# One-hot tiles built block by block with a column of codes as the scalar, and node degrees counted later

## The chip, the cores and the metric

The kernel runs on one NeuronCore of a Trainium2 chip. The metric is device time in microseconds of one execution, from start to end of the program; lower is better. The engines that matter are TensorE (PE), VectorE (DVE), ScalarE (ACT), GpSimd (POOL) and the DMA queue of SyncE (SP). They run side by side, each with its own instruction stream, and meet at semaphores.

## The reference

A graph network on 3125 nodes with 512 features and 53125 directed edges (`src`, `dst`, sorted by `dst`). Two parts, each followed by a residual and a layer norm:

```python
# part 0: three mean-aggregation layers
deg = segment_sum(ones, dst); inv_deg = 1 / clip(deg, 1)
h = x
for l in range(3):
    neigh = segment_sum(h[src], dst) * inv_deg[:, None]
    h = h @ Ws_self[l] + neigh @ Ws_neigh[l] + bs[l]
    if l != 2: h = relu(h)
x = layernorm(x + h)
# part 1: per edge: a filter MLP on 20 attributes, times gathered 4*32 features and
# 4 angular values, summed into the node idx_i = src, two small products, layer norm
```

## The kernel before

The nodes are cut into 25 tiles of 125. Part 0 sums neighbours with a dense adjacency count matrix: for each destination tile a plane of 125 source rows x (25 tiles x 125) in bf16, kept in DRAM as `adj`. The product `h @ Wn` is split into a high and a low f16 half (`table`), so that one aggregation of a tile is 25 x 2 matmuls of 512 columns (line 1122).

**Building the planes.** Edges of five consecutive destination nodes form a block of at most 128 edges; 25 blocks make one destination tile. For each edge there are two codes: the source row within its tile (0 to 124) and source tile x 5 + node within the block (0 to 124). DVE makes for a tile two one-hot arrays of 128 edges x 25 blocks x 125, `oh_b` (`one_hot_rows`, line 1546) and `oh_c` (`one_hot_codes`, line 1552), each in one instruction that compares two broadcast operands. PE multiplies them block by block (line 993, 25 matmuls of 125 columns for a tile, in seven groups in PSUM), ACT evicts each group (line 1253) and SP stores the plane.

**Order of the work.** Three written-out loops set the order on every engine.

- First stage, `for w in range(25)`: node tile w is transposed and multiplied with the first layer's two weight matrices (`product(w, 0)` and `product(w, 1)`, line 964, four steps of 512 columns each). DVE takes the row maximum and scale (lines 1568 to 1574), the low half (line 1581, after ACT's high half of line 1242) and the own part plus bias (`own_part`, line 1607). The plane builder runs `LAG` = 6 node tiles behind: `builder_of(w)` is w - 6. On DVE iteration w makes the one-hots of the tile that PE multiplies in w + 1. On PE the seven groups of blocks stand after the first seven of the eight steps of the two products.
- Aggregation, `for k in range(75)`: k = 0 to 24 is layer 0, and so on. PE does the 50 matmuls of tile k and, in between, the next layer's transposes and products. The last six planes are built here (one-hots in k = 0 to 4). DVE also scales the adjacency plane (`scale`, line 1561), adds mean and own part (`mean_plus_state`, line 1614), and in k = 1 to 17 sorts edges by source for part 1 (`bin_numbers`, `count_bins`, `bin_starts`, `place_bins`, `places_first`, `places_last`).
- Part 1: POOL scatters the sorted edges' rows to DRAM (line 820), and later gathers messages (lines 856 and 825) that DVE, ACT and PE work on.

**The head.** `chunks`, `first_edges`, `codes_first` (w = 2) and `codes_second` (w = 3) make the codes on DVE from rows that POOL gathered. `codes_second` also compares 125 x 3200 values (line 1474) and sums them (line 1476) for the node degrees. SP stores the degrees and reads them back as rows at w = 4, PE transposes them at w = 5 (line 1072), and `degrees_and_rounds` turns them into `inv_deg`. That same function derives from a flag whether a general path is needed (`rounds_i`); each engine then loads this value into a register and branches over the general path (`general`), which these inputs never take. On PE the branch stands ahead of the products of w = 5.

Of the kernel before, what the change touches and what calls it, by code (L numbers as in the profile page):

```python
# [5 lines left out]
BF16 = mybir.dt.bfloat16  # L6
# [5 lines left out]
P = 128  # L12
# [74 lines left out]
def gnn_kernel(nc, x, src, dst, src_n, pay, ws, wn, bs, w_in, w1, b1, w2, b2, wf1, wf2, out):  # L87
# [40 lines left out]
    inv_deg = sb("inv_deg", [P, TILES])  # L128
    deg_row = sb("deg_row", [TILES, TN])
# [23 lines left out]
    place_i = sort.take(P, [CH], I32)  # L153
    early = Region(sort_sb[:, :], 7 * CH * 4)
# [52 lines left out]
    col_b = high.take(P, [GB, EP], BF16)  # L207
    col_c = high.take(P, [GB, EP], BF16)
# [4 lines left out]
    part_b = alias.take(EP, [GB, P])  # L213
    part_c = alias.take(EP, [GB, P])
    in_node = alias.take(EP, [GB, NODES, P], BF16)
    node_deg = alias.take(EP, [GB, NODES])
# [28 lines left out]
    gfirst = pre.take(EP, [GB], I32)  # L245
    falls = oh_b[0].rearrange("p a d -> p (a d)")[0:EP, 0:EC]
# [192 lines left out]
    BLOCKS_AT = (1, 4, 8, 10, 15, 18, 21)  # L439

# [88 lines left out]
    with nc.Block() as block:  # L529

        @block.sync
        def _(sp):
# [96 lines left out]
            for k in range(KC):  # L629
                sp.dma_start(weights[0][:, 0, k, :], wn[0, k * P:(k + 1) * P, :]).then_inc(s_w0[k], 16)  # L630
            load_weights(0, 1)
            load_x(1)
# [4 lines left out]
            for w in range(TILES):  # L637
# [15 lines left out]
                if w == 4:  # L653
                    sp.wait_ge(s_degn, 1)
                    sp.dma_start(bass.AP(degrees.tensor, 0, [[NODES, EP], [NODES * EP, GB], [1, NODES]]), node_deg[:, :, :]).then_inc(s_degst, 16)
                    sp.wait_ge(s_degst, 16)
                    sp.dma_start(deg_row[:, :], degrees.rearrange("(t d) -> t d", d=TN)).then_inc(s_degld, 16)
# [262 lines left out]
        def _(pe):  # L920
# [61 lines left out]
            def multiply_blocks(tb, j):  # L982

                if j == 0:
                    pe.wait_ge(s_ohb, tb + 1)
                    pe.wait_ge(s_ohc, tb + 1)
# [9 lines left out]
            def transpose_codes():  # L996
                pe.wait_ge(s_codes, 1)
                for g in range(GB - 1):
                    pe.transpose(p_b[0][:, g * EP:(g + 1) * EP], part_b[:, g, :], ident[0:EP, 0:EP])
                    last = pe.transpose(p_b[1][:, g * EP:(g + 1) * EP], part_c[:, g, :], ident[0:EP, 0:EP])  # L1000
                last.then_inc(s_ctp[0], 1)
                pe.wait_ge(s_cols, 2)
                pe.transpose(p_b[0][:, 0:EP], part_b[:, GB - 1, :], ident[0:EP, 0:EP])
                pe.transpose(p_b[0][:, P:P + EP], part_c[:, GB - 1, :], ident[0:EP, 0:EP])
                pe.matmul(p_b[1][0:1, 0:1], flags[0:EP, 2:3], ones32[0:EP, 0:1], start=True, stop=True).then_inc(s_ctp[1], 1)
# [59 lines left out]
            for w in range(TILES):  # L1065
                if w + 1 < TILES:
                    transpose_x(w + 1)
                tb = builder_of(w)
                if w == LAG - 1:
                    pe.wait_ge(s_meta, 1)  # L1070
                    pe.wait_ge(s_degld, 16)
                    pe.transpose(p_b[1][0:TN, 0:TILES], deg_row[:, :], ident[0:TILES, 0:TILES]).then_inc(s_degt, 1)
                    general(pe, general_counts)

                def blocks_between(step):
                    if tb is not None and step < PARTS:
                        multiply_blocks(tb, step)

                product(w, 0, blocks_between)
                product(w, 1, blocks_between)  # L1080
                if w == LAG - 2:
                    transpose_codes()
# [146 lines left out]
        def _(act):  # L1229
# [25 lines left out]
            def columns():  # L1255
                act.wait_ge(s_ctp[0], 1)
                for b, col in enumerate((col_b, col_c)):
                    act.activation(col[:, 0:GB - 1, :], p_b[b][:, 0:(GB - 1) * EP].rearrange("p (g e) -> p g e", e=EP), ACT.Copy).then_inc(s_cols, 1)
                act.wait_ge(s_ctp[1], 1)
                for b, col in enumerate((col_b, col_c)):  # L1260
                    act.activation(col[:, GB - 1, :], p_b[0][:, b * P:b * P + EP], ACT.Copy).then_inc(s_cols, 1)

            transposed(0, ACT.Copy)
            for w in range(TILES):
                if w + 1 < TILES:
                    transposed(w + 1, ACT.Copy)
                if w == LAG - 2:
                    columns()
# [4 lines left out]
                row_hi(w)  # L1273

# [722 lines left out]
```

## Time and profile before

| | |
|---|---|
| median of 3 runs | 1993.61 us (1992.96 to 1994.01) |
| profiled execution | 1993.22 us |
| its span, first to last instruction | 1991.4 us |
| outside the span | 1.8 us |
| PE busy | 1870.8 us (94%) |
| DVE busy | 1284.2 us (64%) |
| POOL busy | 1088.7 us (55%) |
| ACT busy | 591.3 us (30%) |
| mean granted TensorE clock | 0.978 |

A row of a timeline gives the start, the duration, the engine, the source line, the operation, what is written and read, the shapes, and in brackets how long the engine was idle before it and who ended that. Durations of neighbouring instructions of one engine overlap a little, so the time that an instruction costs its engine is the distance from its start to the next start, called its pitch below. The timeline merges like instructions (x4, x16). A PE product of one step shows as two records.

### The profile page before, as it was taken

How to read it: one execution, taken by the hardware profiler on the slowest of the kernel's cores; microseconds unless marked ns; L12 is line 12 of the kernel's file. 1: busy time of each engine (PE TensorE's matmuls, PEld its weight loads, DVE VectorE, ACT ScalarE, POOL GpSimd, SP SyncE). 2: the span in 40 equal slices, each digit the busy share in tenths (PEclk: the TensorE clock that was granted, in tenths of full speed). 3: DMA queues.
4: the chain of work that ended last, by engine and by line, in shares of the span. 5: the costliest groups of instructions: out<-in, count | busy, mean ns of one | idle time of the engine just before them, and what ended most of it. 6: DMA issues, size and time to landing. Idle time of an engine off the chain costs nothing. (4 is left out here: it accounts for less than half of the span.)

```text
span 1991.4 us, 23719 instructions
## 1 busy us (share of the span) xinstructions
PE 1870.8 (94%) x8447; PEld 1195.1 (60%) x8447; DVE 1284.2 (64%) x1989; ACT 591.3 (30%) x1380; POOL 1088.7 (55%) x1057
## 2 busy tenths in 40 slices
PE   7799989999999999999999999999994988989996
PEld 3344446555555555555555556666663777878885
DVE  6899999767884333333333334555542888989997
ACT  1355533200000000000000000111112767778884
POOL 4000000000007788878887888568887777777773
PEclk9899999999999999999999999999996999999998
DMA  4155454422223324323232324555654334333341
GB/s 148 59 174 183 157 190 149 150 88 68 91 87 110 87 78 136 110 86 95 93 99 83 94 67 140 163 174 193 199 165 129 98 101 119 107 98 112 111 114 49
DMA packets 112345, 236.72 MB, mean 119 GB/s; under 512 B 28406, under 2 KB 52627, under 8 KB 112224
## 3 DMA queue, kind: packets, MB, share of 16 engines
q1 hardware_dynamic: 77152, 179.50, 27.6%
q0 software_dynamic: 35072, 55.66, 10.4%
q8 instruction: 70, 1.15, 0.2%
q14 instruction: 51, 0.42, 0.1%
HBM read 159.94 MB, written 75.11 MB: 118 GB/s over the span
## 5 line engine op out<-in xcount | busy, mean ns | idle before, releaser
L1122 PE MATMUL low<-table,abuf 125*125 125x512 f16 x3750 | 845.7, 380 | 4.8 <-DVE abuf L1561 4.8
L1122 PEld LDWEIGHTS low<-table,abuf 125*125 125x125 bf16 x3750 | 506.1, 137 | 301.1 <-issue 29.4
L964 PE MATMUL mid<-wbuf,h_t 128*125 128x512 f32 x1200 | 558.7, 602 | 4.3 <-DVE st_out L1607 2.8
L820 POOL DMA_INDIRECT by_src<-scat_row,sort x416 | 487.5, 1172 | 126.1 <-issue 118.9
L825 POOL DMA_INDIRECT table<-msg_table,wbuf x294 | 315.5, 1073 | 91.0 <-issue 87.6
L964 PEld LDWEIGHTS mid<-wbuf,h_t 128*125 128x125 f32 x1200 | 214.4, 189 | 208.7 <-issue 198.9
L812 POOL TENSOR_TENSOR scat_row<-scat_row 128x64 f32<-128x64 f32 x26 | 16.1, 618 | 557.2 <-DVE sort L1727 556.7
L1156 PE MATMUL low<-table,wbuf 128*125 128x256 f32 x900 | 220.4, 396 | 56.4 <-DVE table L1857 55.9
L1614 DVE SCALAR_TENSOR_TENSOR y<-low,inv_deg,st_in 125x512 f32<-125x512 f32 x75 | 56.3, 750 | 326.0 <-PE low L1122 205.7
L1561 DVE TENSOR_TENSOR abuf<-abuf,row_scale 125x3125 bf16<-125x3125 bf16 (+3 forms) x84 | 256.5, 3059 | 3.5 <-DMA abuf<-adj 3.5
L1238 ACT ACTIVATE h_t<-mid 128x500 f32<-128x500 f32 x100 | 58.5, 585 | 583.2 <-PE mid L934 436.9
L1156 PEld LDWEIGHTS low<-table,wbuf 128*125 128x125 f32 x900 | 173.3, 196 | 90.6 <-DVE table L1857 60.5
L856 POOL DMA_INDIRECT sort<-msg_table,sort x156 | 185.3, 1188 | 60.5 <-issue 60.5
L1242 ACT ACTIVATE table<-mid,row_inv 125x512 f16<-125x512 f32 x75 | 51.5, 686 | 427.7 <-DVE row_inv L1573 427.7
L1568 DVE TENSOR_REDUCE row_max<-mid 125x1 f32<-125x512 f32 x75 | 51.6, 688 | 175.2 <-PE mid L964 174.8
L1351 ACT ACTIVATE table<-table,wbuf 128x128 f32<-128x128 f32 x450 | 139.3, 388 | 58.6 <-DVE table L1845 57.6
L1253 ACT ACTIVATE table<-top 125x500 bf16<-125x500 f32 (+1 forms) x175 | 117.2, 693 | 98.5 <-PE top L993 98.2
L993 PEld LDWEIGHTS top<-table 128*125 128x125 bf16 x625 | 59.4, 138 | 92.7 <-issue 56.0
L1134 PE MATMUL mid<-w_sb,wbuf 97*128 97x384 f32 (+2 forms) x450 | 112.7, 387 | 2.3 <-issue 2.3
L1581 DVE SCALAR_TENSOR_TENSOR table<-mid,row_inv,table 125x512 f16<-125x512 f32 x75 | 56.3, 751 | 56.8 <-ACT table L1242 54.6
L1546 DVE TENSOR_TENSOR table<-table,node_iota 128x3125 bf16<-128x3125 bf16 x25 | 85.2, 3407 | 2.2 <-issue 2.2
L1552 DVE TENSOR_TENSOR table<-table,node_iota 128x3125 bf16<-128x3125 bf16 x25 | 85.2, 3408 | 0.0
(214 smaller groups left out, 1658.1 us busy)
## 6 DMA issues: line engine op xcount, KB each, us to landing
abuf<-adj SPq DMA_DIRECT2D x75, 781.2 KB, 4.8
adj<-table SPq DMA_DIRECT2D x25, 781.2 KB, 4.6
states<-st_out SPq DMA_DIRECT2D x75, 256.0 KB, 2.0
st_in<-states SPq DMA_DIRECT2D x75, 256.0 KB, 4.9
table<-early_rows SPq DMA_DIRECT2D x25, 384.0 KB, 6.7
early_rows<-sort POOLq DMA_DIRECT2D x24, 384.0 KB, 3.2
by_src<-scat_row,sort POOLq DMA_INDIRECT x416, 2.2
by_src<-blank SPq DMA_DIRECT2D x25, 252.0 KB, 4.4
```

The costliest lines, as they stand in the source:

```text
L820: pool.indirect_dma_start(out=by_src, out_offset=bass.IndirectOffsetOnAxis(ap=place_i[:, k * PIECE + j:k * PIECE + j + 1], axis=0), in_=sc ...
L825: pool.indirect_dma_start(out=rows[:, j, :], out_offset=None, in_=msg_table[:, :], in_offset=bass.IndirectOffsetOnAxis(ap=win[:, j, PAY_DS ...
L856: pool.indirect_dma_start(out=e_rows[s % 3][:, j, :], out_offset=None, in_=msg_table[:, :], in_offset=bass.IndirectOffsetOnAxis(ap=idx, ax ...
L964: last = pe.matmul(to[0:TN, :], h_t[i % 2][:, k, :], weights[l % 2][:, a, k, :], start=k == 0, stop=k == KC - 1)
L1122: last = pe.matmul(p_agg[k % 2][0:TN, :], a_tile[k % 3][:, a, :], table[ps % 2][0:TN, a, h, :], start=a == 0 and h == 0, stop=a == TILES - ...
L1134: last = pe.matmul(w[:, (b * BLK + lo) * G:(b * BLK + hi) * G], filters[b], w2_sb[:, lo:hi, :].rearrange("k a b -> k (a b)"), start=True, ...
L1156: last = pe.matmul(p_acc[0:TN, :], hot32[:, g * GS + j, :], msg[n % 2][:, j, :], start=g == 0 and j == 0, stop=g == NG - 1 and j == GS - 1)
L1253: act.activation(to, of, ACT.Copy).then_inc(s_blke, 1)
L1351: last = act.activation(msg[n % 2][:, j, 0:G], av[n % 2][:, j, :], ACT.Copy, scale=win_p[t % 3][:, g * GS + j, PAY_Y:PAY_Y + 1])
L1546: dve.tensor_tensor(oh_b[tb % 2], col_b.rearrange("p g e -> p (g e)")[:, tb * BLOCKS:(tb + 1) * BLOCKS].unsqueeze(2).broadcast_to([P, BLOC ...
L1552: dve.tensor_tensor(oh_c[tb % 2], col_c.rearrange("p g e -> p (g e)")[:, tb * BLOCKS:(tb + 1) * BLOCKS].unsqueeze(2).broadcast_to([P, BLOC ...
L1561: dve.tensor_tensor(a_tile[k % 3][:, lo:hi, :], a_tile[k % 3][:, lo:hi, :], row_scale[k // TILES % 2][0:TN, lo:hi].unsqueeze(2).broadcast_ ...
```

## The change

1. `one_hot_rows` and `one_hot_codes` no longer issue one instruction of 128 x 3125 each, but 25 instructions of 128 x 125 each: the block's column of codes (`col_b`, `col_c`, `col_last`, now float32) is the scalar operand of a `tensor_scalar` against `node_iota`. The semaphore is raised by the last of the 25.
2. The two degree instructions leave `codes_second` and run at w = 9 and w = 10; the store and load of the degrees move on SP from w = 4 to w = 12 and 13, the PE transpose and the two small DVE instructions to w = 14.
3. On PE and ACT the transposes of the codes and their evictions are spread: first part at the end of w = 4, second part between the two products of w = 5; the branch of PE stands after both products of w = 5. `rounds` on DVE needs only the flag.
4. On PE the seven groups of blocks stand after steps 0, 1, 3, 4, 5, 6, 7.
5. `bin_numbers` uses other scratch tiles, and its memset moves to `bin_starts` (k = 7). `load_x(1)` is issued ahead of the second weight load. The general path keeps its degrees in `inv_far`, copied later.

```diff
             def one_hot_rows(tb):
                 if tb >= 2:
                     dve.wait_ge(s_blk, PARTS * (tb - 1))
-                dve.tensor_tensor(oh_b[tb % 2], col_b.rearrange("p g e -> p (g e)")[:, tb * BLOCKS:(tb + 1) * BLOCKS].unsqueeze(2).broadcast_to([P, BLOCKS, TN]),
-                                  node_iota[:, :].unsqueeze(1).broadcast_to([P, BLOCKS, TN]), ALU.is_equal).then_inc(s_ohb, 1)
+                if tb == (GB - 1) * EP // BLOCKS:
+                    dve.wait_ge(s_cols, 4)
+                for b in range(BLOCKS):
+                    n = tb * BLOCKS + b
+                    last = dve.tensor_scalar(oh_b[tb % 2][:, b, :], node_iota[:, :], col_b[:, n:n + 1], None, ALU.is_equal)
+                last.then_inc(s_ohb, 1)
...
+                for b in range(BLOCKS):
+                    n, m = tb * BLOCKS + b, tb * BLOCKS + b - (GB - 1) * EP
+                    code = col_c[:, n:n + 1] if m < 0 else col_last[:, m:m + 1]
+                    last = dve.tensor_scalar(oh_c[tb % 2][:, b, :], node_iota[:, 0:CODES], code, None, ALU.is_equal)
+                last.then_inc(s_ohc, 1)
...
+            def in_nodes():
...
+            def degrees():
                 dve.tensor_reduce(node_deg[:, :, :], in_node[:, :, :, :], AX.X, ALU.add).then_inc(s_degn, 1)
...
+            def rounds():
+                dve.wait_ge(s_ctp[0], 1)
+                ch.link(dve.tensor_scalar(flags[0:1, 3:4], p_agg[0][0:1, 0:1], 1.0, float(TILES), ALU.min, ALU.mult))
                 ch.link(dve.tensor_scalar(rounds_i[0:1, 1:2], flags[0:1, 3:4], 1.0, None, ALU.add))
                 dve.sem_inc(s_meta, 1)
+
+            def mean_factors():
                 dve.wait_ge(s_degt, 1)
...
             for w in range(TILES):
                 if w == LAG - 1:
-                    degrees_and_rounds()
+                    rounds()
                     general(dve, general_counts)
-                    dve.wait_ge(s_cols, 4)
+                    dve.wait_ge(s_cols, 2)
...
+                if w == LAG + 3:
+                    in_nodes()
+                if w == LAG + 4:
+                    degrees()
+                if w == LAG + 8:
+                    mean_factors()
```

On PE:

```diff
+    BLOCK_STEPS = (0, 1, 3, 4, 5, 6, 7)
...
+                if w == LAG + 8:
+                    pe.wait_ge(s_degld, 16)
+                    pe.transpose(p_agg[1][0:TN, 0:TILES], deg_row[:, :], ident[0:TILES, 0:TILES]).then_inc(s_degt, 1)
+
+                def blocks_between(step):
+                    if tb is not None and step in BLOCK_STEPS:
+                        multiply_blocks(tb, BLOCK_STEPS.index(step))
+
+                product(w, 0, blocks_between)
+                if w == LAG - 1:
+                    codes_second()
+                product(w, 1, blocks_between)
+                if w == LAG - 2:
+                    codes_first()
                 if w == LAG - 1:
                     pe.wait_ge(s_meta, 1)
-                    pe.wait_ge(s_degld, 16)
-                    pe.transpose(p_b[1][0:TN, 0:TILES], deg_row[:, :], ident[0:TILES, 0:TILES]).then_inc(s_degt, 1)
                     general(pe, general_counts)
```

## Rows read from the trace of the kernel before

**Rows 1.** Stages: busy us of PE, PEld, DVE, ACT, POOL; clock, DMA share, GB/s.
```profile
100.00:150.00 50.00, 46.63 (x221) 22.89 (x220) 46.15 (x49) 27.75 (x45) 0.00 (x0) 1.00 0.53 174
800.00:1000.00 200.00, 200.00 (x776) 113.49 (x775) 75.71 (x110) 14.01 (x22) 160.73 (x154) 1.00 0.32 97
```
**Rows 2.** Timeline of DVE over one node tile of the first stage.
```profile
91.27 3.41 DVE L1546 TENSOR_TENSOR table<-table,node_iota 128x3125 bf16<-128x3125 bf16 x1
...
97.92 0.68 DVE L1568 TENSOR_REDUCE row_max<-mid 125x1 f32<-125x512 f32 x1
...
101.43 3.41 DVE L1546 TENSOR_TENSOR table<-table,node_iota 128x3125 bf16<-128x3125 bf16 x1
```
**Rows 3.** Timeline of PE: transposes ahead of w = 6 and 7, first aggregation.
```profile
78.25 0.59 PE L927 MATMUL mid<-ident,st_in 125*128 125x125 f32 x4
...
87.36 0.59 PE L927 MATMUL mid<-ident,st_in 125*128 125x125 f32 x4
...
273.77 0.65 PE L1122 MATMUL low<-table,abuf 125*125 125x512 f16 x2 [4.77 <-DVE abuf L1561]
```
**Rows 4.** Groups of DVE instructions by line and shape: count, busy us, mean ns.
```profile
L1581 DVE SCALAR_TENSOR_TENSOR table<-mid,row_inv,table 125x512 f16<-125x512 f32 x75 | 56.3, 751 | 56.8 <-ACT table L1242 54.6 <-issue 2.1
L1607 DVE TENSOR_TENSOR st_out<-mid,bias 125x512 f32<-125x512 f32 x75 | 51.5, 686 | 15.0 <-PE mid L964 15.0
L1631 DVE TENSOR_SCALAR table<-y,mv,rstd 125x512 f32<-125x512 f32 x25 | 13.7, 547 | 3.8 <-ACT rstd L1280 3.8
L1462 DVE TENSOR_SCALAR table<-table 125x640 f32<-125x640 f32 x1 | 0.5, 495 | 0.0
```
**Rows 5.** Timeline of DVE at small instructions and at ones with pointer scalars.
```profile
5.93 0.29 DVE L1437 TENSOR_SCALAR abuf<-ident,abuf 125x125 f32<-125x125 f32 x1
6.13 0.60 DVE L1438 TENSOR_TENSOR table<-abuf 125x425 bf16<-125x425 f32 x1
...
26.83 0.15 DVE L1573 TENSOR_SCALAR row_inv<-row_inv_i 125x1 f32<-125x1 f32 x1
26.91 0.14 DVE L1574 TENSOR_SCALAR row_scale<-row_pow 125x1 f32<-125x1 f32 x1
...
1225.04 0.54 DVE L1631 TENSOR_SCALAR table<-y,mv,rstd 125x512 f32<-125x512 f32 x1
1225.50 0.68 DVE L1620 TENSOR_TENSOR st_in<-st_in,st_out 125x512 f32<-125x512 f32 x1
```
**Rows 6.** Timeline of DVE in the head, from degrees to the first one-hots.
```profile
54.17 3.49 DVE L1474 TENSOR_TENSOR table<-table,node_iota 125x3200 bf16<-125x3200 f32 x1
...
61.09 0.68 DVE L1568 TENSOR_REDUCE row_max<-mid 125x1 f32<-125x512 f32 x1
...
64.79 0.14 DVE L1481 TENSOR_SCALAR rounds_i<-flags 1x1 int32<-1x1 f32 x1
68.23 0.18 DVE L1484 TENSOR_SCALAR deg_t<-top 125x25 f32<-125x25 f32 x1 [3.30 <-PE top L1072]
...
70.93 3.42 DVE L1546 TENSOR_TENSOR table<-table,node_iota 128x3125 bf16<-128x3125 bf16 x1 [2.17 <-issue]
```
**Rows 7.** Timeline of PE in the head.
```profile
67.81 0.37 PE L1072 MATMUL top<-ident,deg_row 25*125 25x25 f32 x1 [9.44 <-DMA deg_row<-degrees]
```
**Rows 8.** Timeline of DVE, k = 0 to 4, at ends of iterations.
```profile
287.93 0.75 DVE L1614 SCALAR_TENSOR_TENSOR y<-low,inv_deg,st_in 125x512 f32<-125x512 f32 x1 [0.27 <-PE low L1122]
...
306.70 0.75 DVE L1581 SCALAR_TENSOR_TENSOR table<-mid,row_inv,table 125x512 f16<-125x512 f32 x1 [2.15 <-issue]
...
328.62 0.74 DVE L1614 SCALAR_TENSOR_TENSOR y<-low,inv_deg,st_in 125x512 f32<-125x512 f32 x1
...
349.27 0.74 DVE L1614 SCALAR_TENSOR_TENSOR y<-low,inv_deg,st_in 125x512 f32<-125x512 f32 x1
```
**Rows 9.** Timelines: PE transposing y in k = 5; POOL's first scatter work.
```profile
370.72 0.65 PE L934 MATMUL mid<-ident,y 125*128 125x125 f32 x4 [0.88 <-DVE y L1614]
...
598.00 0.32 POOL L812 TENSOR_TENSOR scat_row<-scat_row 128x64 f32<-128x64 f32 x1 [556.71 <-DVE sort L1727]
```

More of the change, by code:

```diff
@@ L128, in gnn_kernel @@
     inv_deg = sb("inv_deg", [P, TILES])
+    inv_far = sb("inv_far", [P, TILES])
     deg_row = sb("deg_row", [TILES, TN])
@@ L153, in gnn_kernel @@
     place_i = sort.take(P, [CH], I32)
+    cols = Region(sort_sb[:, :], 7 * CH * 4)
+    cols.at = 4 * CH * 4
+    col_b = cols.take(P, [N // NODES])
+    col_c = cols.take(P, [(GB - 1) * EP])
+    col_last = sb("col_last", [P, EP])
     early = Region(sort_sb[:, :], 7 * CH * 4)
@@ L212, in gnn_kernel @@
     part_a = alias.take(EP, [GB, P])
[L213 to L216, printed above, removed]
+    part_b = alias.take(EP, [GB, P], at=5 * 4 * D + 4 * 6272)
+    part_c = alias.take(EP, [GB, P], at=5 * 4 * D + 4 * 6272 + 2560)
     alias.at = 5 * 4 * D
@@ L245, in gnn_kernel @@
     gfirst = pre.take(EP, [GB], I32)
+    in_node = pre.take(EP, [GB, NODES, P], BF16, at=4096)
+    node_deg = pre.take(EP, [GB, NODES], at=4096 + 6400)
     falls = oh_b[0].rearrange("p a d -> p (a d)")[0:EP, 0:EC]
@@ L630, in _ @@
                 sp.dma_start(weights[0][:, 0, k, :], wn[0, k * P:(k + 1) * P, :]).then_inc(s_w0[k], 16)
+            load_x(1)
             load_weights(0, 1)
-            load_x(1)
             for to, of in biases[0:1]:
@@ L984, in multiply_blocks @@
                 if j == 0:
+                    if tb == 0:
+                        pe.wait_ge(s_cols, 4)
                     pe.wait_ge(s_ohb, tb + 1)
@@ L1253, in evict_blocks, with columns_first, columns_second @@
                 act.activation(to, of, ACT.Copy).then_inc(s_blke, 1)
-            def columns():
+            def columns_first():
                 act.wait_ge(s_ctp[0], 1)
-                for b, col in enumerate((col_b, col_c)):
-                    act.activation(col[:, 0:GB - 1, :], p_b[b][:, 0:(GB - 1) * EP].rearrange("p (g e) -> p g e", e=EP), ACT.Copy).then_inc(s_cols, 1)
+                act.activation(col_b[:, 0:(GB - 1) * EP], p_b[0][:, 0:(GB - 1) * EP], ACT.Copy).then_inc(s_cols, 1)
+                act.activation(col_c[:, :], p_b[1][:, 0:(GB - 1) * EP], ACT.Copy).then_inc(s_cols, 1)
+            def columns_second():
                 act.wait_ge(s_ctp[1], 1)
-                for b, col in enumerate((col_b, col_c)):
-                    act.activation(col[:, GB - 1, :], p_b[0][:, b * P:b * P + EP], ACT.Copy).then_inc(s_cols, 1)
+                act.activation(col_b[:, (GB - 1) * EP:GB * EP], p_b[0][:, 0:EP], ACT.Copy).then_inc(s_cols, 1)
+                act.activation(col_last[:, :], p_b[0][:, P:P + EP], ACT.Copy).then_inc(s_cols, 1)
             transposed(0, ACT.Copy)
@@ L1266, in _ @@
                     transposed(w + 1, ACT.Copy)
-                if w == LAG - 2:
-                    columns()
+                if w == LAG - 1:
+                    columns_second()
                 tb = builder_of(w)
@@ L1273, in _ @@
                 row_hi(w)
+                if w == LAG - 2:
+                    columns_first()
             def root(k, var=s_var, done=s_rstd):
@@ L1670, in bin_starts @@
                 dve.wait_ge(s_pre, 1)
+                ch.link(dve.memset(place_f[:, :], 0.0))
                 ch.link(dve.tensor_copy(totals[:, :], p_b[0][:, 64:64 + BINS]))
```

53 lines of the change are left out of this document (21 added, 32 removed).

## The prediction

> **What bounds the kernel now.** I read the busy time by stage first, then the timelines of DVE and PE where no engine is plainly full, then the groups of DVE instructions for prices. From about 400 us on, PE is busy without a gap [rows 1], so nothing that DVE saves or loses there counts. In the first stage both PE (46.6 of 50 us) and DVE (46.2 of 50) look nearly full, and only the timeline tells which sets the pace. DVE goes from one pair of one-hots to the next in 101.43 - 91.27 = 10.16 us: 97.92 - 91.27 = 6.65 us for the pair, 3.51 us for scales, low half and own part, which include a 0.75 us wait for ACT [rows 2, 4]. PE needs 87.36 - 78.25 = 9.11 us for w = 6, where DVE was ahead [rows 3]. So DVE sets the pace from w = 6 to 24, by 1.05 us a tile, and PE then waits 4.77 us for the first scaled plane [rows 3]. This goes on into the aggregation: DVE's iterations k = 2 and 3 take 349.27 - 328.62 = 20.65 us with no idle, and in k = 5 PE still waits 0.88 us for y [rows 8, 9]. After that PE is the bound. POOL's scatter begins when DVE has the places in k = 17 (598 us) [rows 9], and that iteration follows PE, so a time lost or won before k = 5 moves everything behind it by the same amount, the gathers of the tail included.
>
> **The one-hots.** Removed for each of 25 planes: two instructions, together 6.65 us, that is 0.133 us for each of the 50 blocks-and-codes [rows 2]. Added: 50 small ones. Their price p has three parts.
> - Fixed part. Two independent one-element instructions start 26.91 - 26.83 = 0.08 us apart, with a duration of 0.15 [rows 5]. The pitch is the duration less about 0.08.
> - Pointer scalar. L1462, with constants as scalars, takes 495 ns for 640 columns of f32 and L1574 144 ns for one [rows 4, 5]: 0.55 ns a column. By that L1631 (512 columns) would take 425 ns; it takes 547 with two pointer scalars, so 61 ns each. L1581, which has one pointer and reads PSUM, takes 751 against 686 of L1607 with none [rows 4]: 65 ns. It is in the pitch too: L1631 follows its predecessor at once and holds the engine for 1225.50 - 1225.04 = 0.46 us, where 425 ns of duration would make 0.35 [rows 5]. I take 0.06.
> - Columns. 125 of them: nothing at best, 125 x 0.55 = 0.07 us at the f32 rate. The nearest row, L1437 (125 columns of f32, one pointer), has a pitch of 6.13 - 5.93 = 0.20 [rows 5], in line with 0.08 + 0.06 + 0.07. No row has a bf16 `tensor_scalar`. I take 0.03, half of the f32 rate, in the middle between the ends.
>
> So p = 0.17 us (0.14 to 0.21), against 0.133 now. The broadcast instruction paid one fixed cost for 25 blocks, and its one element per 1.06 ns costs 0.13 us a block; the new form streams faster but pays 0.14 us before its first column. A pair becomes 50 x 0.17 = 8.5 us: +1.85 us. All 25 pairs lie where DVE sets the pace: +46.3 us.
>
> The Trainium skill (VectorE: DVE Perf Modes, the perf-mode tier table) gives a bf16 `tensor_scalar` from SBUF to SBUF four elements a cycle and an f32 one two. By that the columns would be 0.033 us and the sum nearly the same; no trace row of before shows the bf16 form.
>
> **Degrees.** The two instructions of 54.17 to 61.09 (6.92 us) [rows 6] leave the head, where DVE is the last to finish before the first one-hots, and return at w = 9 and 10, again on DVE, which sets the pace there: -6.9 and +6.9. The two small ones (68.23 to 68.77) move likewise, 0. What is really saved is the wait between them: DVE reached 64.93 (the end of L1481) and got the degrees at 68.23, behind the store and load of the degrees and PE's transpose, for which PE itself stood 9.44 us [rows 6, 7]: -3.3 us. The 2.17 us in which DVE loads the branch value stays [rows 6]. At w = 12 to 14 the same two transfers stand in SP's queue; they took about 6.7 us from 61.1 to 67.8 with both waits [rows 6, 7], and a tile is then 12 us, so PE's wait at w = 14 ends before its products are due. Queued behind it would be the blocks of w = 14; PE has 12.0 - 9.1 = 2.9 us of slack a tile.
>
> **Codes and branch between products, order of the groups.** These relieve PE and ACT, and both have slack under a DVE of 12.0 us a tile: 0. If DVE did not set the pace, they would be worth what the faster rival says below. `load_x(1)` earlier: the head up to 54 us waits for POOL's gathers and DVE's work on them, 0. The memset moved to k = 7, where DVE waits for PE: at most -0.4, within the covers below.
>
> **Covers.** DVE idles 0.27 us ahead of y in k = 0 and 2.15 us in k = 1, where line 1581 waits for ACT behind PE's last group [rows 8]. The longer one-hots use them up: -2.4, with the memset -2.8.
>
> **Sum.** 46.3 - 3.3 - 2.8 = +40.2 us. Against the profiled execution, 1993.22 (its span 1991.4 and 1.8 outside; 0.4 below the median 1993.61): 2033 us. What shows first: DVE's tile 12.0 us, PE starting the first aggregation some 25 x 1.85 less the last five = 20 x 1.85 - 3.3 = 34 us later, near 307, then another 6 us to k = 5.
> With p = 0.14: 25 x 0.35 = 8.75, sum +2.7, 1996 us. With p = 0.21: 25 x 3.85 = 96.3, sum +90, 2083 us.
>
> **Rivals.**
> - Faster: the pointer is read while the instruction before still streams, when many follow each other. Then p = 0.08 + 0.03 = 0.11, a pair 5.5 us, DVE's tile 9.0, and PE's 9.11 sets the pace; it decides below p = (9.11 - 3.51) / 50 = 0.112, and any gain at all needs p below 0.14. Then PE starts w = 6 some 12 us earlier (9.4 of waiting, the rest its slow restart), 18 tiles gain 1.04 each (-19), the degrees push DVE behind PE for one time (+6), the 4.77 us shrink by 2.5 and k = 4 and 5 lose 1.4: -29, 1964 us. For it: no row has two pointer instructions of this size in a row. Against: L1631 had its predecessor's 3.3 us to hide in and didn't. In the Trainium skill, the Vector Engine (DVE) Microarchitecture Reference (section 5.2) puts a built-in one-source operation at its columns plus about 75 ns, with no charge for a pointer, and would give this case's time; the 0.08 agrees with it, L1631 doesn't.
> - Odd rows of 125 bf16 elements stream at one element per cycle, as the broadcast form did (0.13 us a block): p = 0.08 + 0.06 + 0.13 = 0.27, a pair 13.5, 25 x 6.85 = 171, sum +165, 2158 us. Against: L1437 has 125 columns too, and 0.20 leaves no room for 0.13 beside a pointer.
> - No measurable change: p near 0.14, so that the 3.3 us and the covers pay for it, 1996 us. Decides below p = 0.141. It would need columns that cost nothing.
> - The f32 rate for bf16: p = 0.21, 2083 us; it is the upper end of my case.
>
> **Chances.** My case, slower by the price of 1250 small instructions: 0.76 (p 0.145 to 0.21). One element per cycle: 0.02. No change, within 0.2% (4 us, about what a measurement of this kernel can tell): 0.05. Faster, pointer hidden: 0.17. The range leaves out the fast rival and the slowest: 1996 to 2083. Faster 0.17, same 0.05, slower 0.78.
>
> **What would show it.** L1546's and L1552's successors: duration near 0.25 us, pitch 0.17 within a run of 25. DVE's tile in the first stage near 12.0 us, PE idle some 2.9 us in each, ahead of its first block group. First one-hot near 60 us, 70.93 - 6.92 - 3.3 - 0.54. Two instructions of 3.5 us at w = 9 and 10. No wait for `deg_row` on PE beyond a microsecond. From k = 6 on the same iterations as now, shifted. The prediction is wrong if the pitch in a run is at or below 0.13: the time then falls, and PE's order of groups and branch begins to matter; it is also wrong if PE, idling more often, gets a lower clock and drops behind DVE.

## The result, and the profile after

The changed kernel takes 2024.7 us (median of 4 runs, 2022.79 to 2025.91); the kernel before took 1993.28 us on the same chip. The ratio is 1.0155 (95% interval 1.0143 to 1.0167), +31.4 us. The profiled execution took 2024.31 us (span 2022.5), 31.1 more than the profiled one of before. Where some executions of a kernel below fell into a second, slower state of the chip, its time and ratio are those of the others.

The head first, in the timeline of DVE:

```profile
53.71 0.68 DVE L1597 TENSOR_REDUCE row_max<-mid 125x1 f32<-125x512 f32 x1
...
57.40 0.14 DVE L1501 TENSOR_SCALAR rounds_i<-flags 1x1 int32<-1x1 f32 x1
59.47 4.29 DVE L1572 TENSOR_SCALAR table<-node_iota,sort 128x125 bf16<-128x125 bf16 x25 [1.93 <-issue]
```

Only the load of the branch value (1.93 us) now stands between that value and the one-hots. The 3.30 us in which DVE waited for the degrees in [rows 6] are gone, and the one-hots start 11.46 us earlier than at 70.93. Then tiles of the first stage, the same timeline:

```profile
71.28 4.17 DVE L1572 TENSOR_SCALAR table<-node_iota,sort 128x125 bf16<-128x125 bf16 x25
75.35 4.17 DVE L1581 TENSOR_SCALAR table<-node_iota,sort 128x125 bf16<-128x125 bf16 x25
79.42 0.69 DVE L1597 TENSOR_REDUCE row_max<-mid 125x1 f32<-125x512 f32 x1
...
82.95 3.19 DVE L1572 TENSOR_SCALAR table<-node_iota,sort 128x125 bf16<-128x125 bf16 x19
...
117.93 3.48 DVE L1492 TENSOR_TENSOR abuf<-table,node_iota 125x3200 bf16<-125x3200 f32 x1
121.45 4.18 DVE L1572 TENSOR_SCALAR table<-node_iota,sort 128x125 bf16<-128x125 bf16 x25
...
133.12 3.48 DVE L1496 TENSOR_REDUCE abuf<-abuf 125x25 f32<-125x3200 bf16 x1
```

An array of 25 instructions takes 75.35 - 71.28 = 4.07 us, so the pitch is 0.163 us. A pair takes 79.42 - 71.28 = 8.14 us where it took 6.65 [rows 2], and a tile 82.95 - 71.28 = 11.67 where it took 10.16. The two degree instructions stand at w = 9 and 10, on DVE as before. DVE has no other idle time in a tile than its 0.75 us for ACT.

PE now idles in nearly every tile, ahead of the first group of blocks. Two of the 16 gaps, of 31.8 us together, that the profile puts on line 1001 as "issue" stand in PE's timeline:

```profile
79.62 0.45 PE L1001 MATMUL top<-table 128*125 128x125 bf16 x4 [2.31 <-issue]
79.87 2.01 PE L970 MATMUL mid<-wbuf,h_t 128*125 128x512 f32 x2
...
91.29 0.41 PE L1001 MATMUL top<-table 128*125 128x125 bf16 x4 [0.75 <-issue]
91.54 1.07 PE L970 MATMUL mid<-wbuf,h_t 128*125 128x512 f32 x2
...
300.06 1.11 PE L1134 MATMUL low<-table,abuf 125*125 125x512 f16 x2 [6.61 <-DVE abuf L1590]
...
402.64 0.65 PE L940 MATMUL mid<-ident,y 125*128 125x125 f32 x4 [0.86 <-DVE y L1643]
...
421.79 0.59 PE L940 MATMUL mid<-ident,y 125*128 125x125 f32 x4
```

The first aggregation starts at 300.06 (273.77 in [rows 3]). The k = 5 transposes of y start at 402.64, with the same short wait as at 370.72 in [rows 9]: +31.92. In k = 6 PE is at 421.79 with no gap, and the kernel before was there at 389.86, as this line of its PE timeline shows:

```profile
389.86 0.59 PE L934 MATMUL mid<-ident,y 125*128 125x125 f32 x4
```

That is +31.93, so PE no longer waits for y, and nothing is won or lost between k = 5 and k = 6. POOL's scatter begins at 629.93 against 598.00 [rows 9], again +31.93. From k = 6 to the end the changed kernel takes 1600.7 us and the kernel before 1601.5, so the end is +31.1. What a version is worth can therefore be read at the start of the y transposes in k = 6.

The view by stage, after (columns as in [rows 1]):

```profile
100.00:150.00 50.00, 37.59 (x156) 18.95 (x155) 46.42 (x214) 19.57 (x31) 0.00 (x0) 0.86 0.38 127
800.00:1000.00 200.00, 200.00 (x777) 113.43 (x776) 76.72 (x112) 14.02 (x22) 161.05 (x153) 1.00 0.32 98
```

PE's busy time in the stage falls from 46.6 to 37.6 us while DVE's stays at 46; DVE sets the pace more clearly than before. The stretch from 800 us on is unchanged.

### The profile page after: what moved, and what is told of

It reads as the page before. It is cut to its first block and busy times, and to the rows that moved or that the text cites. A ratio compares the mean times of both kernels' runs of the same rounds, so it can differ in the third digit from the quotient of the medians.

```text
span 2022.5 us, 24921 instructions
## 1 busy us (share of the span) xinstructions
PE 1883.9 (93%) x8447; PEld 1203.9 (60%) x8447; DVE 1322.2 (65%) x3189; ACT 592.5 (29%) x1380; POOL 1092.9 (54%) x1057
## 5 line engine op out<-in xcount | busy, mean ns | idle before, releaser
L970 PE MATMUL mid<-wbuf,h_t 128*125 128x512 f32 x1200 | 570.8, 614 | 5.5 <-DVE st_out L1636 5.5
L970 PEld LDWEIGHTS mid<-wbuf,h_t 128*125 128x125 f32 x1200 | 220.3, 193 | 215.8 <-issue 204.0
L1572 DVE TENSOR_SCALAR table<-node_iota,sort 128x125 bf16<-128x125 bf16 x625 | 104.2, 250 | 2.0 <-issue 1.9
L1001 PE MATMUL top<-table 128*125 128x125 bf16 x625 | 68.5, 229 | 33.9 <-issue 31.8
```

What stands on the lines that cost most here:

```text
L970: last = pe.matmul(to[0:TN, :], h_t[i % 2][:, k, :], weights[l % 2][:, a, k, :], start=k == 0, stop=k == KC - 1)
L1001: last = pe.matmul(p_b[n % 2][0:TN, b * CODES:(b + 1) * CODES], oh_b[tb % 2][:, first + b, :], oh_c[tb % 2][:, first + b, :], start=True, ...
L1572: last = dve.tensor_scalar(oh_b[tb % 2][:, b, :], node_iota[:, :], col_b[:, n:n + 1], None, ALU.is_equal)
```

## The experiments

All kernels below are compared with the kernel before on their own chip. Four of them (the pairs of blocks, in their first two forms, on both bases) ran on chips where the kernel before itself took 2108 to 2111 us; why those chips were slower was not looked into. Of these four only ratios, differences within one chip and traces up to k = 6 are used.

**1. The other parts of the change alone.** The changed kernel, with the two broadcast instructions and their bf16 columns of codes back:

```diff
-                for b in range(BLOCKS):
-                    n = tb * BLOCKS + b
-                    last = dve.tensor_scalar(oh_b[tb % 2][:, b, :], node_iota[:, :], col_b[:, n:n + 1], None, ALU.is_equal)
-                last.then_inc(s_ohb, 1)
+                dve.tensor_tensor(oh_b[tb % 2], col_b[:, tb * BLOCKS:(tb + 1) * BLOCKS].unsqueeze(2).broadcast_to([P, BLOCKS, TN]),
+                                  node_iota[:, :].unsqueeze(1).broadcast_to([P, BLOCKS, TN]), ALU.is_equal).then_inc(s_ohb, 1)
```

> The changed kernel with the one-hots as before: one instruction of 128 x 3125 for each array. Theory (the small one-hots are the whole loss, the other parts are worth the 3.3 us of waiting that they take out of the head): DVE's tile back at 10.16 us, first one-hots near 59.5 us, two degree instructions of 3.5 us at w = 9 and 10, time 1988 to 1991 us. Rival (the other parts cost time themselves, by the degrees in the stage where DVE sets the pace or by PE's order of groups): 1996 us or more.

Measured: 1990.29 us against 1992.43, ratio 0.9992 (0.9982 to 1.0002). The loss is gone with the small instructions. The rest of the change, with DVE as the bound, is worth 2 us by the medians, which can't be told from nothing, and nothing by the trace: its first one-hots start at 62.47, and PE transposes y in k = 6 at 390.09, where the kernel before stood at 389.86. Its DVE and PE timelines:

```profile
62.47 3.42 DVE L1570 TENSOR_TENSOR table<-sort,node_iota 128x3125 bf16<-128x3125 bf16 x1 [2.17 <-issue]
...
390.09 0.59 PE L940 MATMUL mid<-ident,y 125*128 125x125 f32 x4
```

**2. The small one-hots alone**, in the kernel before, with the columns of codes in float32. The columns' new place also brings along the other scratch tiles of `bin_numbers` and the moved memset (point 5 of the change):

```diff
-                dve.tensor_tensor(oh_b[tb % 2], col_b.rearrange("p g e -> p (g e)")[:, tb * BLOCKS:(tb + 1) * BLOCKS].unsqueeze(2).broadcast_to([P, BLOCKS, TN]),
-                                  node_iota[:, :].unsqueeze(1).broadcast_to([P, BLOCKS, TN]), ALU.is_equal).then_inc(s_ohb, 1)
+                for b in range(BLOCKS):
+                    n = tb * BLOCKS + b
+                    last = dve.tensor_scalar(oh_b[tb % 2][:, b, :], node_iota[:, :], col_b[:, n:n + 1], None, ALU.is_equal)
+                last.then_inc(s_ohb, 1)
```

> The kernel before with the small one-hots alone: degrees, branch, codes and order of groups stay as before. Theory: 25 pairs by 1.5 us is 37.4, less 2.8 us of covers in k = 0 and 1: 2028 us, 3 us above the changed kernel. Rival (the small one-hots cost less where DVE has no degrees in between, and the other parts hold a share of the loss): 2015 us or less.

Measured: 2027.91 us, ratio 1.0182 (1.0168 to 1.0196), +35.5 us. The one-hots are the whole loss: without the rest of the change it is 4 us larger than with it (35.5 against 31.4, each against its own measurement of the kernel before).

**3. What is in the 0.163 us.** First a constant in place of the pointer. This version leaves out the comparison with the codes, so its adjacency counts are not those of the graph:

```diff
-                    last = dve.tensor_scalar(oh_b[tb % 2][:, b, :], node_iota[:, :], col_b[:, n:n + 1], None, ALU.is_equal)
+                    last = dve.tensor_scalar(oh_b[tb % 2][:, b, :], node_iota[:, :], float(b), None, ALU.is_equal)
```

> The changed kernel with a constant in place of the column of codes as the scalar of all 1250 small instructions; the comparison with the codes is left out, so the adjacency counts are not those of the graph. Theory (the pointer costs 0.06 us of each pitch): pitch 0.10 to 0.11 us, a pair 5.2, DVE's tile 8.8 us or less, PE sets the pace at 9.1 us a tile, no wait of PE for the first block group, time 1960 to 1970 us. Rival (the small instruction itself costs 0.16 us, whatever its scalar): pitch 0.16, tile 11.7, 2024 us.

Measured: 1960.56 us, ratio 0.9844 (0.9829 to 0.9859). Its DVE timeline:

```profile
68.55 2.65 DVE L1572 TENSOR_SCALAR table<-node_iota 128x125 bf16<-128x125 bf16 x25
71.11 2.65 DVE L1581 TENSOR_SCALAR table<-node_iota 128x125 bf16<-128x125 bf16 x25
...
77.18 1.01 DVE L1572 TENSOR_SCALAR table<-node_iota 128x125 bf16<-128x125 bf16 x9
```

The array takes 2.56 us, 0.1025 each, and the tile 8.63 us. The pointer alone is 0.163 - 0.1025 = 0.060 us of pitch, and it is all that stands between +31 and -32 us. (With the constant PE sets the pace, so its time no longer shows the whole 1250 x 0.060.) Then the same instruction, pointer and all, with an f32 first operand:

```diff
-                    last = dve.tensor_scalar(oh_b[tb % 2][:, b, :], node_iota[:, :], col_b[:, n:n + 1], None, ALU.is_equal)
+                    last = dve.tensor_scalar(oh_b[tb % 2][:, b, :], node_iota32[:, :], col_b[:, n:n + 1], None, ALU.is_equal)
```

> The changed kernel with the node numbers of the comparison read as float32 instead of bf16, output bf16 as before. Theory (of the pitch of 0.163 us, 0.03 are the 125 columns at four a cycle, and with an operand of four bytes they go at two a cycle): pitch 0.195 us, DVE's tile 13.3 us, 25 pairs by 1.6 us more: 2065 us. Rival (the columns are hidden behind fixed costs): pitch 0.163, 2025 us.

Measured: 2064.0 us, ratio 1.0365 (1.0348 to 1.0381); an array takes 4.86 us in its timeline, 0.194 each. The groups of line 1572 in the three kernels (count, busy us, mean ns): changed kernel, constant, f32. The last view ends at 400 us and so has 600 of the 625.

```profile
L1572 DVE TENSOR_SCALAR table<-node_iota,sort 128x125 bf16<-128x125 bf16 x625 | 104.2, 250 | 2.0 <-issue 1.9
```

```profile
L1572 DVE TENSOR_SCALAR table<-node_iota 128x125 bf16<-128x125 bf16 x625 | 66.4, 188 | 2.1 <-issue 1.9
```

```profile
L1572 DVE TENSOR_SCALAR table<-node_iota,sort 128x125 bf16<-128x125 f32 x600 | 118.6, 278 | 2.0 <-issue 2.0
```

Durations differ by 62 and 28 ns, pitches by 60 and 31. A duration contains some 0.087 us that the next instruction covers, and the differences pass into the pitch whole.

**4. Does the order of PE's groups matter once PE is the bound?** The constant version, where DVE's tile is shorter than PE's, with the seven groups at their old steps:

```diff
-    BLOCK_STEPS = (0, 1, 3, 4, 5, 6, 7)
+    BLOCK_STEPS = (0, 1, 2, 3, 4, 5, 6)
```

> The kernel e3 (constant scalars, comparison with the codes left out) with the groups of blocks after steps 0 to 6 of the products, as before the change. Theory (the third group then waits for ACT's first eviction, which stands behind the high half of the tile before, and with PE as the pace that wait counts): 0.3 to 0.7 us in each of some 17 tiles, 5 to 12 us above e3. Rival (PE's wait is hidden or was only a sign of DVE's pace): within 2 us of e3.

Measured: 1961.76 us, ratio 0.9842 (0.9826 to 0.9858), against 0.9844 with the new steps. The 5 to 12 us that were expected did not come: the order of the groups is worth nothing that can be measured, and PE waits for ACT's evictions 2.6 us in all with the old order.

**5. Fewer, faster instructions: all blocks innermost.** The pointer and the count are the cost of the small form. A `tensor_tensor` whose innermost elements are neighbours might stream faster than the broadcast one and pay neither. Here the node is the outer and the block the inner dimension, in runs of five, against a table that repeats each node number five times:

```diff
+            def packed(to, code):
+                return dve.tensor_tensor(to.rearrange("p d (x y) -> p d x y", y=5),
+                                         code.rearrange("p (x y) -> p x y", y=5).unsqueeze(1).broadcast_to([P, TN, BLOCKS // 5, 5]),
+                                         iota_by_five[:, :, :].unsqueeze(2).broadcast_to([P, TN, BLOCKS // 5, 5]), ALU.is_equal)
...
+                packed(packed_b[tb % 2], col_b[:, tb * BLOCKS:(tb + 1) * BLOCKS]).then_inc(s_ohb, 1)
```

> The changed kernel with another one-hot: one tensor_tensor for each array again, but written node number outermost and block innermost, so that the codes are read with step 1 and the other operand is a table in which each node number stands five times; all operands bf16 with step 1 innermost. PE then reads weights and moving columns at a step of 25 elements. Theory (the broadcast form was slow for its inner step of 0, a bf16 tensor_tensor with step 1 gives two elements per 1.04 ns): 1.7 us an array, DVE's tile 7.0 us, PE sets the pace at 9.1 us a tile if the step of 25 costs it nothing, time 1953 to 1962 us, below both kernels. Rival one (DVE stays at one element a cycle): pitch 3.33 us an array, 1990 us. Rival two (PE pays for the step in its 25 products of blocks): more than 9.1 us a tile, by as much as these products get longer.

Measured: 2062.07 us, ratio 1.0352 (1.0336 to 1.0368). DVE's part came faster, PE's slower. Three views of this kernel: the group of DVE and the group of PE's weight loads (both from 60 to 400 us), and PE's timeline.

```profile
L1569 DVE TENSOR_TENSOR table<-sort,iota_by_five 128x3125 bf16<-128x3125 bf16 x44 | 90.9, 2105 | 2.0 <-issue 1.9
```

```profile
L1003 PEld LDWEIGHTS top<-table 128*125 128x125 bf16 x566 | 165.4, 345 | 45.5 <-issue 32.4
```

```profile
78.34 0.61 PE L935 MATMUL mid<-ident,st_in 125*128 125x125 f32 x4
78.79 1.02 PE L972 MATMUL mid<-wbuf,h_t 128*125 128x512 f32 x2
79.65 1.12 PE L1003 MATMUL top<-table 128*125 128x125 bf16 x4
80.59 1.04 PE L972 MATMUL mid<-wbuf,h_t 128*125 128x512 f32 x2
...
91.66 0.61 PE L935 MATMUL mid<-ident,st_in 125*128 125x125 f32 x4
```

DVE makes an array in 2.1 us (3.41 before). But PE, whose operands now lie 25 elements apart, needs 80.59 - 79.65 = 0.94 us for four blocks, 0.235 each, where the changed kernel's next product followed after 91.54 - 91.29 = 0.25. Its tile is 91.66 - 78.34 = 13.32 us, and PE sets the pace: the second rival of the expectation. The same one-hots in the kernel before:

> The kernel before with the packed one-hots of e5 alone. Theory (with DVE off the pace the other parts of the change count: 3 us of waiting for the degrees, PE's branch and its wait for them, 9 us, and the order of groups, where PE waits 0.67 us in each tile for ACT's first eviction): 15 to 20 us above e5, near 1975 us. Rival (the other parts are worth their 3 us whoever sets the pace): within 5 us of e5.

Measured: 2075.87 us, ratio 1.0416 (1.0401 to 1.0432), 13.8 us above the one before. The expected absolute time missed by 100 us, since it was built on that of the run above, and the difference came out a little short of the expected 15 to 20. Its size still says something: the other parts of the change are worth much more where PE is the bound than the 2 us that they gave where DVE is.

**6. Pairs of blocks.** Two blocks are interleaved: DVE's runs are two elements long, and PE reads its operands at a step of two elements. One instruction makes 24 blocks of an array, one small one the 25th:

```diff
+            def one_hot(to, oh, code):
+                dve.tensor_tensor(to, code[:, 0:PAIRED].rearrange("p (x y) -> p x y", y=2).unsqueeze(2).broadcast_to([P, PAIRED // 2, TN, 2]),
+                                  iota_by_two[:, :, :].unsqueeze(1).broadcast_to([P, PAIRED // 2, TN, 2]), ALU.is_equal)
+                return dve.tensor_tensor(oh[:, PAIRED, :], code[:, PAIRED:PAIRED + 1].broadcast_to([P, TN]), node_iota[:, :], ALU.is_equal)
...
-                    last = pe.matmul(p_b[n % 2][0:TN, b * CODES:(b + 1) * CODES], oh_b[tb % 2][:, first + b, :], oh_c[tb % 2][:, first + b, :], start=True, stop=True)
+                    x, y = divmod(first + b, 2)
+                    rows, cols_of = ((q[tb % 2][:, x, :, y] if first + b < PAIRED else oh[tb % 2][:, first + b, :]) for q, oh in ((pairs_b, oh_b), (pairs_c, oh_c)))
+                    last = pe.matmul(p_b[n % 2][0:TN, b * CODES:(b + 1) * CODES], rows, cols_of, start=True, stop=True)
```

> The changed kernel with one-hots in pairs of blocks: one tensor_tensor makes 24 blocks as 12 pairs, written node number by node number with the two blocks of a pair side by side (node table with each number twice), a second small one makes block 25; PE reads its operands at a step of two elements. Theory (DVE gets its two elements per 1.04 ns from runs of two as well, and PE, which paid at a step of 25, reads both elements of four bytes at full rate): 1.85 to 2.3 us an array, DVE's tile 7.2 to 8.1 us, PE's products of four blocks 0.39 us as before, PE sets the pace at 9.1 us, time 1953 to 1963 us, below both kernels. Rival (any step but one costs PE): its tile 10 us or more, 1985 us or more.

Its time can't be compared across chips. Measured: 2077.08 us where the kernel before took 2111.20, ratio 0.9861 (0.9803 to 0.9919). The timeline of its DVE shows two speeds of the same instruction:

```profile
85.76 3.27 DVE L1572 TENSOR_TENSOR table<-sort,iota_by_two 128x3000 bf16<-128x3000 bf16 x1
...
96.03 1.71 DVE L1572 TENSOR_TENSOR table<-sort,iota_by_two 128x3000 bf16<-128x3000 bf16 x1
```

A tile has 25 codes of two bytes, so every second tile's codes start 2 bytes off a 4-byte boundary, and the two speeds alternate by tile. A slow tile takes DVE 96.03 - 85.76 = 10.27 us, more than PE's 9.1. The same on the kernel before:

> The kernel before with the paired one-hots of e8 alone. Theory (with DVE off the pace the other parts of the change are worth what they take off PE: 9.4 us of standing for the degrees and its slow restart after it, less what the degrees cost at w = 9 and 10): e8 plus 8 to 13 us. Rival (they are worth the 3 us that e1 showed, whoever sets the pace): e8 plus 3 us.

Measured: 2089.47 us, ratio 0.9932 (0.9886 to 0.9978). By the medians that is 12.4 us above its partner, as the theory has it, but the intervals of the two ratios overlap, and the traces don't bear it out. These are the y transposes of k = 6, in the changed kernel with pairs and in the kernel before with pairs:

```profile
364.59 0.59 PE L943 MATMUL mid<-ident,y 125*128 125x125 f32 x4
```

```profile
368.79 0.59 PE L937 MATMUL mid<-ident,y 125*128 125x125 f32 x4
```

The other parts of the change are worth 4.2 us here, near the rival's 3. The rest of the difference arises after k = 6, where the two kernels do the same work and still took 1709 and 1720 us on this chip. That DVE still set the pace in the slow tiles, so that PE could make up part of its waits, would explain the small gain; it was not tested by itself. To test the reading of the two speeds, each tile's codes get 26 columns:

```diff
-    col_b = cols.take(P, [N // NODES], BF16)
+    col_b = cols.take(P, [TILES, BLOCKS + 1], BF16)
...
+                one_hot(pairs_b[tb % 2], oh_b[tb % 2], col_b[:, tb, 0:BLOCKS]).then_inc(s_ohb, 1)
```

> The kernel e8 with the codes kept at 26 columns for each tile instead of 25, so that every tile's codes begin on four bytes. In e8 the large instruction took 1.71 us for planes with an even number and 3.27 us for odd ones, whose codes begin two bytes off. Theory (the odd start is the cause): 1.71 us for all 50; DVE's tile 7.2 us for odd and even alike, PE sets the pace at 9.1 us; time 1954 to 1962 us where the kernel before has 1992, ratio 0.981 to 0.985. Rival (another cause that goes with the plane's number, such as the buffer): 1.71 and 3.27 alternate as in e8.

Measured: 2075.24 us against 2108.05, ratio 0.985 (0.9805 to 0.9896). All 50 large instructions are fast now, and the y transposes of k = 6 come 10.3 us earlier than with the two speeds (364.59, then 354.31 below); the two ratios are too wide to show it. The group by shape:

```profile
L1571 DVE TENSOR_TENSOR table<-sort,iota_by_two 128x3000 bf16<-128x3000 bf16 x50 | 85.6, 1711 | 2.2 <-issue 2.2
```

And the aligned pairs in the kernel before:

> The kernel before with the paired and aligned one-hots of e10 alone. Theory (with PE as the pace, the other parts of the change are worth PE's standing of 9 us for the degrees and its restart, less up to 3 us that the degrees cost at w = 9 and 10, and more than the 3 us of e1): e10 plus 8 to 14 us, ratio 0.987 to 0.991. Rival (worth 3 us whoever sets the pace): e10 plus 3 us, ratio 0.983 to 0.986.

Measured: 2085.32 us, ratio 0.9897 (0.9844 to 0.995), 10.1 us above its partner by the medians, with intervals that overlap again. By the traces the k = 6 transposes start at 365.44 here and at 354.31 in the partner, 11.1 us apart, and the stretch behind them agrees within 1 us (1717.2 and 1718.1). The PE timelines, first of the kernel before with aligned pairs, then of the changed kernel with them:

```profile
68.00 0.37 PE L1077 MATMUL top<-ident,deg_row 25*125 25x25 f32 x1 [8.00 <-DMA deg_row<-degrees]
69.93 9.43 PE L967 MATMUL mid<-wbuf,h_t 128*125 128x512 f32 x16 [1.57 <-issue]
...
365.44 0.59 PE L937 MATMUL mid<-ident,y 125*128 125x125 f32 x4
```

```profile
354.31 0.59 PE L942 MATMUL mid<-ident,y 125*128 125x125 f32 x4
```

PE's waits for the degrees and for the branch value, 8.00 and 1.57 us, make 9.6 of the 11.1; the changed kernel has neither here. While DVE set the pace PE could make them up, now it can't. The last run is the best version again, on a chip where the kernel before takes 1990 us:

> The kernel with blocks in pairs and codes that start on 4 bytes once more, for its time beside the kernel before on a chip whose memory is less disturbed. The theory (a pair of one-hots costs 4.0 us instead of 6.65 on DVE, PE sets the pace of the first stage): its trace had PE transpose y in k = 6 at 354.31 us where before had 389.86, 35.5 us earlier, and from there on nothing differs between the kernels, so 1993 - 35 = 1958 us, a ratio of 0.982 (0.980 to 0.985). The rival (the kernel gives part of that back later, in the aggregation or in part 1, and the ratio of 0.985 was the true one): 1963 us or more.

Measured: 1958.29 us (1956.69 to 1961.24) against 1990.47, ratio 0.9838 (0.9822 to 0.9855). Its DVE and PE timelines and its view by stage:

```profile
87.09 1.71 DVE L1571 TENSOR_TENSOR table<-sort,iota_by_two 128x3000 bf16<-128x3000 bf16 x1
88.72 0.28 DVE L1573 TENSOR_TENSOR table<-sort,node_iota 128x125 bf16<-128x125 bf16 x1
...
90.75 0.68 DVE L1600 TENSOR_REDUCE row_max<-mid 125x1 f32<-125x512 f32 x1
...
94.92 0.75 DVE L1613 SCALAR_TENSOR_TENSOR table<-mid,row_inv,table 125x512 f16<-125x512 f32 x1 [2.68 <-ACT table L1258]
...
96.19 1.71 DVE L1571 TENSOR_TENSOR table<-sort,iota_by_two 128x3000 bf16<-128x3000 bf16 x1
```

```profile
93.78 0.60 PE L935 MATMUL mid<-ident,st_in 125*128 125x125 f32 x4
...
102.88 0.60 PE L935 MATMUL mid<-ident,st_in 125*128 125x125 f32 x4
...
355.50 0.59 PE L942 MATMUL mid<-ident,y 125*128 125x125 f32 x4
```

```profile
100.00:150.00 50.00, 47.94 (x234) 25.24 (x233) 39.49 (x68) 30.05 (x47) 0.00 (x0) 1.00 0.66 203
```

A pair of one-hots costs 90.75 - 87.09 = 3.66 us instead of 6.65. DVE's wait in a tile has grown from 0.75 to 2.68 us: it now waits for PE, through ACT, and the tile is PE's 9.10. The y transposes of k = 6 stand at 355.50, 34.4 us ahead of the kernel before, and the profiled execution ends 34.9 ahead of the profiled one of before. Those two were not measured side by side; beside this run the medians differ by 32.2. No sizeable part is given back later, and the theory's 1958 us was met. The kernel with a constant, whose pairs take 5.1 us, ends within 3 us of this one with 3.66: below PE's 9.1 us a tile a faster DVE buys almost nothing more.

## Why the prediction was right

Predicted 2033 us (1996 to 2083), slower; measured 2024.7. The mechanism held, and its largest term was too large by nearly a quarter. The terms were these:

- **The bound.** DVE sets the pace from w = 6 to k = 4: shown. The small one-hots alone cost 35.5 us, DVE's tile grew by 1.51 us, and PE idled ahead of its groups of blocks. From k = 5 on all is shifted: +31.92, +31.93 and +31.93 us at three places down to the scatter. One reading was too wide: PE is not busy without a gap from 400 us on (248 of the 300 us from 1500 to 1800 in the kernel before). It did no harm, since that stretch is the same in both kernels.
- **The price, the mis-sized term.** Predicted 0.17 us each, by 0.08 fixed, 0.06 pointer, 0.03 columns. Measured 0.163: 0.1025 without the pointer, 0.060 for the pointer. The pointer term was right, taken from differences of durations of large instructions. Fixed and columns together are 0.1025, not 0.11; no run tells the two apart. The 0.007 us too much, times 1250, are 8.8 us: 25 x 1.50 = +37.5 in place of +46.3, nearly the whole gap between 2033 and 2024.7. At a count of 1250, two digits of a price were not enough.
- **The columns' rate.** 0.031 us more for f32 (0.194 against 0.163). The prediction took 0.03 for bf16 and 0.07 for f32, a difference of 0.04; it came out at 0.031. The Trainium skill (VectorE: DVE Perf Modes, the perf-mode tier table) gives f32 two elements a cycle and bf16 four, a difference of one cycle for four columns; at the 1.06 ns of one element of the broadcast form that is an estimated 0.033 us for 125, and the two runs agree with it.
- **The head.** Predicted -3.3; it was -4.0: the wait of 3.30, 0.24 less for the branch value (1.93 after 2.17), and DVE was 0.46 ahead at 53.71 where it had been at 54.17. The last two can't be put down to the change: this start scatters. In the other traces on the changed base the first one-hots come between 59.65 and 62.47 and the load of the branch value takes 1.91 to 2.17, while those on the kernel before start between 70.93 and 72.06. The degrees left the head and came back at 3.5 us each, as predicted. PE's wait for them at w = 14 was predicted to stay below a microsecond and was 3.04 us; it cost nothing: DVE's tile beside it is 11.67 us, as elsewhere.
- **The covers.** The short idle stretches of DVE in k = 0 and 1. Predicted -2.8, measured some -1.9, from these lines of DVE's timeline (y in k = 0, the low half in k = 1, y in k = 1 to 3):

```profile
315.43 0.75 DVE L1643 SCALAR_TENSOR_TENSOR y<-low,inv_deg,st_in 125x512 f32<-125x512 f32 x1
...
334.13 0.75 DVE L1610 SCALAR_TENSOR_TENSOR table<-mid,row_inv,table 125x512 f16<-125x512 f32 x1 [1.12 <-ACT table L1254]
...
335.39 0.74 DVE L1643 SCALAR_TENSOR_TENSOR y<-low,inv_deg,st_in 125x512 f32<-125x512 f32 x1
...
357.55 0.74 DVE L1643 SCALAR_TENSOR_TENSOR y<-low,inv_deg,st_in 125x512 f32<-125x512 f32 x1
379.70 0.74 DVE L1643 SCALAR_TENSOR_TENSOR y<-low,inv_deg,st_in 125x512 f32<-125x512 f32 x1
```

  The 0.27 us in k = 0 is used up. Of the 2.15 us in k = 1 [rows 8] 1.12 remain, since the longer one-hots delay PE's last group too, and with it ACT; the memset gives 0.56. From k = 2 an iteration takes 22.15 us where it took 20.65: 1.50 each, the bare price of a pair. Sum: 37.5 - 4.0 - 1.9 = 31.6, and a few tenths around the degrees at w = 9, 10 and 14; measured 31.9 at k = 6. The head came out 0.7 better and the covers 0.9 worse than predicted; that these two cancel is luck.
- **Codes, branch, order of the groups at 0 while DVE is the bound.** The other parts together gave 2 us in experiment 1, and 0 by its trace at k = 6, where the head's term alone would be 3.3. That run reached its first one-hots at 62.47, 3.0 us later than the changed kernel, and 2.5 of them were there when the codes were done (55.94, where the changed kernel had 53.44): the scatter of the head again. Beside the small one-hots the same parts gave 4 us (experiment 2). So the sizes of these small terms stay open within a few microseconds. That the parts matter where PE is the bound is shown by two pairs of kernels: 13.8 us (packed) and 11.1 us (aligned pairs, by the traces). In the pair with two speeds it is 4.2. The order of the groups is worth nothing (experiment 4), and in the aligned pair 9.6 of 11.1 are the waits for the degrees and the branch value.
- **The rivals.** The faster one (the pointer hidden in a row of pointer instructions) is excluded: 24 of 25 such instructions follow another, and each costs 0.060 us more than with a constant. Its price for the case was sound: it gave 1964 us for p = 0.11, and the constant version, at p = 0.1025, takes 1960.6. One element per cycle and the full f32 rate are excluded by 0.163; the latter was run and gives 2064, not 2083, because 0.194 and not 0.21 is its price.
- **The Trainium skill against the trace.** Its Vector Engine (DVE) Microarchitecture Reference (section 5.2) has columns plus about 75 ns and no charge for a pointer. With the 0.033 us for the columns from above that is an estimated 0.108 us. The constant version agrees with it (0.1025), the pointer version (0.163) does not. What the change wanted to escape, the one element per cycle of the broadcast form (3.41 us for 3125), is in the same page's section 5.1: a two-source operation with one element read many times runs at the single rate, and double rate wants innermost runs of at least two. The pairs that start on 4 bytes agree with it: 1.71 us for 3000. The condition is not the whole of it: two bytes off, the same runs of two took 3.27 us, and runs of five took 2.11 for 3125.

## What to carry to other kernels

Before one wide instruction is cut into many, multiply the difference of the two prices by the count, and price the scalar operand too: a pointer instead of a constant cost 0.060 us here, more than half of what the instruction cost without it. When a broadcast operand holds an engine at one element per cycle, look first at the order of the innermost elements; runs of two that began on 4 bytes halved the time, still with one large instruction an array, and the other engine that reads the result decides how far apart the elements may lie. Work that is moved off an engine with slack is worth nothing until the engine beside it becomes faster: the same edits gave 2 and 4 us where DVE set the pace and 11 to 14 where PE did. And where a chip's times scatter, compare two kernels at a point of their traces ahead of the disturbance, not by their medians alone.

## What the runs showed of the hardware

- A pointer scalar adds 0.060 us of pitch to a `tensor_scalar` of 128 x 125 bf16, in an uninterrupted run of 25 as well.
- A bf16 `tensor_tensor` that reads its first operand in runs of two took 1.71 us when the operand began on 4 bytes and 3.27 us when it began 2 bytes off, for 3000 elements per partition. With padded codes, so that each tile's began on 4 bytes, all 50 took 1.71. Runs of five took 2.11 us for 3125, in between and alike in all tiles (2.10 to 2.12), whether their codes began on 4 bytes or two off; why was not tried.
- PE read bf16 operands at a step of two elements at no cost (weight loads of 139 ns in the last run, 138 in the kernel before), and at a step of 25 almost four times as slowly (0.94 against 0.25 us for four blocks, with weight loads of 345 ns).
- TensorE's granted clock in the changed kernel: the view by stage has 0.86 of 2.4 GHz on average from 100 to 150 us, where [rows 1] has 1.00. For most of the stage PE's gaps alternated, 2.31 and 0.75 us. After the gap of 2.31 that ended at 79.62 the next two product instructions took 2.01 us, nearly double, and the granted clock from 79.6 to 82.0 us was 0.56, near the lower of the two levels (1.2 of 2.4 GHz); from 84.0 to 91.2 it was 1.00 again. After the gap of 0.75 that ended at 91.29 they took 1.07. From its first group to the next tile's transposes PE took 9.46 us after the long gap and 7.90 after the short one. The slow products thus cost PE 1.56 us, so that it came back later and found its operands 0.75 us away instead of 2.31. PE's slack under DVE hid all of it here. Where PE is nearer the bound such a gap would cost its own length and the slow products behind it; no run here was made for that.
